# Graph attention and routed experts: a batch's moments placed ahead of the residual's, and the mask load issued inside the norms

## The chip, the cores and the metric

The kernel runs on one core of a Trainium2 chip. The metric is the time of one execution on the device in microseconds (us), as the median of several runs. The core has five instruction streams that this text names: TensorE (PE in the rows), VectorE (DVE), ScalarE (ACT), GpSimd (POOL) and SyncE (SP, which only issues transfers). They run beside one another and wait for one another through semaphores.

## The reference, cut to what matters

For each of 16 batches of 512 rows with 128 features:

```
xn   = layernorm(x)                          # first norm
Wh   = xn @ W.T;  si, sj = Wh @ a1, Wh @ a2
e    = leaky_relu(si[:, None] + sj[None, :], 0.2)
att  = softmax(where(adj > 0, e, -9e15))
x1   = x + elu(att @ Wh)                     # first residual
x2   = layernorm(x1)                         # second norm
rw   = softmax(mean over tokens of x2 @ Wr + br), rescaled, softmax again
out  = x1 + layernorm(x2 + sum over the top 2 experts of gate * (gelu(x2 @ W1 + b1) @ W2 + b2)) * gamma + beta
```

`adj` is an int32 matrix of 512 x 512 for every batch.

## The kernel before, in words

Partitions hold rows: a batch is four tiles of 128 rows. The program has two phases. Phase one runs the attention of the 16 batches and keeps x1 and the transposed x2 in SBUF. Then comes a short routing stage, and phase two runs the two chosen experts of each batch. The change touches phase one only.

Phase one is a software pipeline written out by hand, one list of calls per engine and step. `pipeline` writes some first steps out, puts steps 6 to 11 into a hardware loop (two steps to an iteration, with semaphore targets and addresses in registers) and writes the last ones out again. In step n each engine works on several batches at once:

- VectorE, step n: `masked_max` of batch n, tiles 2 and 3 (L690, mask plus the spread destination scores, with the row maximum); between them `residual_pos` of batch n-2 (L731); then `residual_neg` of batch n-2 (L739, writes x1), `stats2` of batch n-2 (L749, four BN_STATS that read x1), `stats1` of batch n+3 (L667, four BN_STATS on the coming rows), `make_mask` of batch n+1 (L676), `invert_sums` of batch n-1 (L711), `logits` tile 0 (L702), `normalize` of n-1 (L720), `logits` 1 and 2, `masked_max` of batch n+1 tiles 0 and 1, `logits` tile 3.
- GpSimd, step n: `norms(n + 2)`, `load_adj(n + 2)`, `row_shifts(n)`. `norms` turns the moments of two batches at once, the first norm of batch n+2 and the second norm of batch n-3, into reciprocal deviations (L457 to L485, the power at L485) and the bias nb (L491). It waits for both VectorE moments (semaphores bn1_stats and bn2_stats). `load_adj` (L436) waits until the mask of two batches back is made and issues the transfer of one batch's adj, cast from int32 to bf16 by the transfer. `row_shifts` (L503 to L514) waits for all four maxima of batch n, and works out z_max, shift_neg and shift_pos.
- ScalarE, step n: `copy_xnt` (L1130), `scale_x2` of batch n-3 (L1195, four instructions that need nb), `leaky_part` tiles 0 and 1 (L1154, need shift_neg), `copy_wh` (L1145, needs the first norm), leaky 2, `probs` (L1184, exponentials of the transposed logits), `copy_x2t` (L1202), leaky 3, probs 1 and 2, `exp_h` (L1162), probs 3.
- TensorE, step n: transposes of x2 (L1426) and of the logits (L1435), the spread of destination scores (L1412), transposes of x (L1389), `attend` (L1451), `project` (L1399).
- SyncE: loads of x and stores of x2 within SBUF.

`logits` of tile 0 waits for leaky of tile 0 and for shift_pos; `invert_sums` waits for the last `attend` of batch n-1. Ahead of the pipeline each engine has a head for batch 0: on GpSimd it ends with `load_adj(0, 2)`, `norms(0, 2)`, and the pipeline's first step then does `norms(0, 3)`, `load_adj(0, 3)`, `row_shifts(0, 1)`. The DMA queue of GpSimd carries nothing but adj in phase one.

A helper, `waits_met`, increments a semaphore of the engine's own behind the waits of a step.

Of the kernel before, what the change touches and what calls it, by code (L numbers as in the profile page):

```python
# [22 lines left out]
def batch_at(half, n):  # L23

    h = half + n // 2
    return 2 * h + n % 2, h, n % 2


def gat_moe_kernel(nc, x, adj, gnn_w, gnn_a, w_router, b_router, w1, b1, w2, b2, gamma, beta, out):
# [15 lines left out]
    with ExitStack() as ctx:  # L45
# [214 lines left out]
        def pipeline(engine, step, first, last, lead, lag):  # L260


            lo = first + lead + (first + lead) % 2
            hi = last - lag + 1
            hi -= hi % 2
            for i in range(first, lo):
                step(0, i)
            with engine.Fori(lo // 2, hi // 2) as half:
                step(half, 0)
                step(half, 1)  # L270
            for i in range(hi, last + 1):
                step(0, i)

        def in_range(half, n, last=B - 1):
            return not isinstance(half, int) or 0 <= 2 * half + n <= last
# [7 lines left out]
        FIRST, LAST = -4, 16  # L283
        LEAD, LAG = 10, 5
# [9 lines left out]
        def past(half, b, k):  # L294
            return not isinstance(half, int) or b >= k

        def waits_met(engine):


            engine.sem_inc(s_met[engine.engine], 1)  # L300
# [119 lines left out]
        def _(pool):  # L420
# [9 lines left out]
            def load_adj(half, n):  # L430

                b, h, par = batch_at(half, n)
                if past(half, b, 2):
                    pool.wait_ge(s_mask, b - 1)
                    waits_met(pool)
                nc.gpsimd.dma_start(adj_sb[par][:], adj_dram[b]).then_inc(s_adj[par], 16)  # L436

            def norms(half, n):
# [4 lines left out]
                first = in_range(half, n)  # L443
# [17 lines left out]
                if second:  # L461
                    nc.gpsimd.tensor_tensor(nm2[:], bn[:, 1, :, 1], bn[:, 1, :, 4], ALU.add).then_inc(s_n2, 1)
                pool.wait_ge(s_norm, base + 1)
                nc.gpsimd.tensor_tensor(sums[:, 3, kinds, :], sums[:, 1, kinds, :], sums[:, 1, kinds, :],
                                        ALU.mult).then_inc(s_norm, 1)
                pool.wait_ge(s_norm, base + 3)
                waits_met(pool)
                nc.gpsimd.tensor_scalar(sums[:, 2, kinds, :], sums[:, 2, kinds, :], 1.0 / D, LN_EPS, ALU.mult,
# [76 lines left out]
            def step(half, n):  # L545
                if in_range(half, n + 2, KEPT - 1 + NORM_LAG):
                    norms(half, n + 2)
                if in_range(half, n + 2) and past(half, n + 2, 2):
                    load_adj(half, n + 2)
                if in_range(half, n):  # L550
                    row_shifts(half, n)

# [7 lines left out]
            row_shifts(0, 0)  # L560
            load_adj(0, 2)
            norms(0, 2)
            pipeline(pool, step, 1, LAST, LEAD + FIRST - 1, LAG)
            pool.wait_ge(s_rw, 64)
            nc.gpsimd.tensor_scalar(br_sb[:], br_sb[:], float(N), 0.0, ALU.mult, ALU.add).then_inc(s_br, 1)
            norm2_third_last()
# [75 lines left out]
        def _(dve):  # L642
# [26 lines left out]
            def make_mask(half, n):  # L669

                b, h, par = batch_at(half, n)
                dve.wait_ge(s_adj[par], 16 * h + 16)
                if past(half, b, 1):
                    dve.wait_ge(s_md, T * b)
                waits_met(dve)
                nc.vector.tensor_scalar(mask[:], adj_sb[par][:], 0.0, -MASKED, ALU.is_le, ALU.mult).then_inc(s_mask, 1)  # L676
# [57 lines left out]
            def residual_neg(half, n):  # L734
                b, h, par = batch_at(half, n)
                dve.wait_ge(s_hexp, b + 1)
                dve.wait_ge(s_x1, 2 * b + 1)
                waits_met(dve)
                nc.vector.scalar_tensor_tensor(out=x1_all[:, b, :], in0=h_exp[:], scalar=1.0, in1=x1_part[:],  # L739
                                               op0=ALU.min, op1=ALU.add).then_inc(s_x1, 1)  # L740
# [36 lines left out]
            def step(half, n):  # L777
                if in_range(half, n):
                    masked_max(half, n, 2)
                if in_range(half, n - 2, B - 2):  # L780
                    residual_pos(half, n - 2)
                if in_range(half, n):
                    masked_max(half, n, 3)
                if in_range(half, n - 2, B - 2):
                    residual_neg(half, n - 2)
                if in_range(half, n - 2, END - 1):
                    stats2(half, n - 2)
                if in_range(half, n + 3):
                    stats1(half, n + 3)
                if in_range(half, n + 1):  # L790
                    make_mask(half, n + 1)
                if in_range(half, n - 1, B - 2):
                    invert_sums(half, n - 1)
                if in_range(half, n):
                    logits(half, n, 0)
                if in_range(half, n - 1, B - 2):
                    normalize(half, n - 1)
                if in_range(half, n):
                    logits(half, n, 1)
                if in_range(half, n):  # L800
                    logits(half, n, 2)
                if in_range(half, n + 1):
                    masked_max(half, n + 1, 0)
                if in_range(half, n + 1):
                    masked_max(half, n + 1, 1)
                if in_range(half, n):
                    logits(half, n, 3)
# [880 lines left out]
```

## Time and profile before

| what | value |
|---|---|
| median of 3 runs | 298.2 us (296.28 to 299.17) |
| the profiled execution, its own time | 298.8 us |
| its span, first to last instruction | 297.1 us |
| mean granted TensorE clock | 0.978 of full |
| PE busy | 260.7 us (88%) |
| DVE busy | 240.9 us (81%) |
| ACT busy | 229.7 us (77%) |
| POOL busy | 174.0 us (59%) |

The shares are means over two phases with different limits, so they do not say what bounds phase one. In the rows below, times count from the span's start. A row of the timeline gives the start, the length, the engine, the line, the operation with its tiles, how many instructions are merged into it, and in brackets how long the engine stood idle before it and which producer ended that.

### The profile page before, as it was taken

How to read it: one execution, taken by the hardware profiler on the slowest of the kernel's cores; microseconds unless marked ns; L12 is line 12 of the kernel's file. 1: busy time of each engine (PE TensorE's matmuls, PEld its weight loads, DVE VectorE, ACT ScalarE, POOL GpSimd, SP SyncE). 2: the span in 40 equal slices, each digit the busy share in tenths (PEclk: the TensorE clock that was granted, in tenths of full speed). 3: DMA queues.
4: the chain of work that ended last, by engine and by line, in shares of the span. 5: the costliest groups of instructions: out<-in, count | busy, mean ns of one | idle time of the engine just before them, and what ended most of it. 6: DMA issues, size and time to landing. Idle time of an engine off the chain costs nothing. (4 is left out here: it accounts for less than half of the span.)

```text
span 297.1 us, 7856 instructions
## 1 busy us (share of the span) xinstructions
PE 260.7 (88%) x1958; PEld 236.5 (80%) x1959; DVE 240.9 (81%) x689; ACT 229.7 (77%) x498; POOL 174.0 (59%) x392
## 2 busy tenths in 40 slices
PE   7585988998889888988898798999999999999990
PEld 5475978888879787978787685689999999999990
DVE  4595899999999999999889877466678787678766
ACT  2384678999988998899889775778779888788670
POOL 3688387787778777788845951123343244432375
PEclk9998699999999999999999899999999999999998
DMA  6998406337575577468500000465465555556313
GB/s 105 182 295 157 71 3 106 58 92 174 108 135 128 125 143 172 98 139 158 107 18 23 35 1 36 151 207 161 143 196 169 196 155 171 177 176 194 107 38 106
DMA packets 47069, 37.26 MB, mean 125 GB/s; under 512 B 2848, under 2 KB 41152, under 8 KB 47040
## 3 DMA queue, kind: packets, MB, share of 16 engines
q1 hardware_dynamic: 38176, 27.49, 29.1%
q0 software_dynamic: 8864, 9.45, 21.6%
q8 instruction: 11, 0.18, 0.2%
q14 instruction: 18, 0.15, 0.1%
HBM read 29.57 MB, written 4.20 MB: 114 GB/s over the span
## 5 line engine op out<-in xcount | busy, mean ns | idle before, releaser
L1451 PE MATMUL banks<-whx,prob_t 128*128 128x129 f32 x512 | 65.9, 278 | 0.0
L1451 PEld LDWEIGHTS banks<-whx,prob_t 128*128 128x128 f32 x512 | 62.1, 195 | 0.0
L1435 PE MATMUL banks<-ident,logit 128*128 128x128 f32 x256 | 40.7, 292 | 21.3 <-DVE logit L702 21.0
L1154 ACT ACTIVATE leaky<-masked_dst,shift_neg 128x512 f32<-128x512 f32 x64 | 44.7, 724 | 12.6 <-POOL shift_neg L513 12.6
L1435 PEld LDWEIGHTS banks<-ident,logit 128*128 128x128 f32 x256 | 29.5, 147 | 29.1 <-DVE logit L702 20.7
L702 DVE SCALAR_TENSOR_TENSOR logit<-masked_dst,shift_pos,leaky 128x512 f32<-128x512 f32 x64 | 46.9, 744 | 3.7 <-POOL shift_pos L514 2.1
L1184 ACT ACTIVATE prob_t<-banks 128x512 f32<-128x512 f32 x64 | 37.0, 609 | 11.0 <-PE banks L1435 10.9
L690 DVE CUSTOM_DVE_ANT_0 masked_dst<-mask,banks 128x512 f32<-128x512 bf16 x64 | 42.2, 682 | 2.1 <-PE banks L1412 1.0
L1320 ACT ACTIVATE logit<-logit,nb,rstd 128x128 f32<-128x128 f32 x60 | 24.8, 484 | 14.7 <-POOL nb L612 14.7
L607 POOL TENSOR_SCALAR veps<-mv 128x4 f32<-128x4 f32 x15 | 5.8, 387 | 48.4 <-DVE mv L1021 44.4
L1624 PEld LDWEIGHTS banks<-w2s,masked_dst 128*128 128x128 f32 x256 | 29.7, 192 | 1.2 <-issue 0.7
L1624 PE MATMUL banks<-w2s,masked_dst 128*128 128x128 f32 x256 | 30.0, 275 | 0.3 <-ACT w2s L1339 0.3
L1609 PE MATMUL banks<-x2t_hi,w_pair 128*128 128x512 f32 x64 | 26.8, 419 | 0.5 <-DMA w_pair<-w_parts 0.5
L1624 PEld LDWEIGHTS banks<-w2s,leaky 128*128 128x128 f32 x224 | 26.1, 192 | 0.6
L1624 PE MATMUL banks<-w2s,leaky 128*128 128x128 f32 x224 | 26.1, 275 | 0.0
L1003 DVE TENSOR_TENSOR logit<-banks,x_all 128x512 f32<-128x512 f32 x15 | 10.4, 691 | 19.2 <-ACT logit L1320 12.7
L485 POOL TENSOR_TENSOR rstd<-sums,minus_half 128x8 f32<-128x8 f32 (+1 forms) x17 | 24.6, 1449 | 1.4 <-ACT whx L1145 0.6
L1611 PE MATMUL banks<-x2t_hi,w_pair 128*128 128x512 f32 x64 | 25.3, 395 | 0.0
L1610 PE MATMUL banks<-x2t_lo,w_pair 128*128 128x512 f32 x64 | 24.9, 389 | 0.0
L1330 ACT ACTIVATE masked_dst<-banks,b_sel 128x512 f32<-128x512 f32 x32 | 19.7, 676 | 3.2 <-PE banks L1611 2.4
L1330 ACT ACTIVATE leaky<-banks,b_sel 128x512 f32<-128x512 f32 x32 | 19.8, 678 | 2.6 <-PE banks L1611 2.5
L1412 PE MATMUL banks<-ident,whx 128*128 128x128 f32 x128 | 19.3, 296 | 2.8 <-ACT whx L1145 2.5
(172 smaller groups left out, 580.4 us busy)
## 6 DMA issues: line engine op xcount, KB each, us to landing
adj_sb<-in_adj_dram POOLq DMA_DIRECT2D x16, 512.0 KB, 7.2
w_pair<-w_parts SPq DMA_DIRECT2D x31, 256.0 KB, 2.5
x_all<-in_x_dram SPq DMA_DIRECT2D x16, 256.0 KB, 4.6
w2r<-in_L_ffn_W_dram SPq DMA_DIRECT2D x32, 128.0 KB, 2.1
out_dram<-prob_t SPq DMA_DIRECT2D x15, 256.0 KB, 2.3
x_all<-x2s SPq DMA_DIRECT2D x13, 256.0 KB, 5.1
x_rows<-in_x_dram SPq DMA_DIRECT2D x8, 256.0 KB, 2.9
w_parts<-in_L_ffn_W_dram SPq DMA_DIRECT2D x1, 1024.0 KB, 8.8
```

What stands on the lines that cost most here:

```text
L690: nc.vector.tensor_tensor_reduce(out=masked_dst[:, t, :], in0=mask[:, t, :], in1=dst_ps, scale=1.0, scalar=-3e38, op0=ALU.add, op1=ALU.max ...
L702: nc.vector.scalar_tensor_tensor(out=logit[:, t, :], in0=masked_dst[:, t, :], scalar=shift_pos[:, t:t + 1], in1=leaky[:, t, :], op0=ALU.ad ...
L1154: nc.scalar.activation(leaky[:, t, :], masked_dst[:, t, :], ACT.Identity, bias=shift_neg[:, t:t + 1], scale=ALPHA).then_inc(s_leaky, 1)
L1184: nc.scalar.activation(prob_t[:, t, :], lt_ps[t % 2], ACT.Exp).then_inc(s_prob, 1)
L1320: nc.scalar.activation(zn[par][:, tile], zs[par][:, tile], ACT.Identity, bias=nb3[par][:, t:t + 1], scale=rstd3[par][:, t:t + 1]).then_inc ...
L1330: nc.scalar.activation(hidden[par][:, kc, :], hid_ps[kc], ACT.Gelu, bias=b1_sel[:, c, bass.ds(b * TOP_K + k, 1)]).then_inc(s_hid, 1)
L1435: last = nc.tensor.transpose(lt_ps[t % 2][:, c * P:(c + 1) * P], logit[:, t, c * P:(c + 1) * P], ident[:])
L1451: last = nc.tensor.matmul(into[:, 0:D + 1], prob_t[:, t, c * P:(c + 1) * P], whx[par][:, c, 2:WHX], start=(c == 0), stop=(c == T - 1))
L1609: nc.tensor.matmul(hid_ps[kc], lo, x2t_hi[par][:], start=True, stop=False)
L1610: nc.tensor.matmul(hid_ps[kc], hi, x2t_lo[par][:], start=False, stop=False)
L1611: nc.tensor.matmul(hid_ps[kc], hi, x2t_hi[par][:], start=False, stop=True).then_inc(s_hid_ps, 1)
L1624: last = nc.tensor.matmul(y_ps[par][:, t * D:(t + 1) * D], hidden[par][:, kc, t * P:(t + 1) * P], w2s[par][:, kc // FC, kc % FC, :], start ...
```

## The change

Three edits, two on GpSimd and one on VectorE. (1) From batch 4 on, `load_adj` of a batch is called inside `norms` of the same batch, behind the square (L464), and no longer between `norms` and `row_shifts`. (2) The first pipeline step of GpSimd is written out: `load_adj(0, 3)` stands behind `row_shifts(0, 1)`. (3) On VectorE `stats1` of batch n+3 is called ahead of `stats2` of batch n-2.

```diff
@@ norms
                 nc.gpsimd.tensor_tensor(sums[:, 3, kinds, :], sums[:, 1, kinds, :], sums[:, 1, kinds, :],
                                         ALU.mult).then_inc(s_norm, 1)
+                if first and past(half, n, 4):
+                    load_adj(half, n)
                 pool.wait_ge(s_norm, base + 3)
@@ step of GpSimd
                     norms(half, n + 2)
-                if in_range(half, n + 2) and past(half, n + 2, 2):
-                    load_adj(half, n + 2)
                 if in_range(half, n):
                     row_shifts(half, n)
@@ head of GpSimd
             norms(0, 2)
-            pipeline(pool, step, 1, LAST, LEAD + FIRST - 1, LAG)
+            norms(0, 3)
+            row_shifts(0, 1)
+            load_adj(0, 3)
+            pipeline(pool, step, 2, LAST, LEAD + FIRST - 2, LAG)
@@ step of VectorE
                     residual_neg(half, n - 2)
+                if in_range(half, n + 3):
+                    stats1(half, n + 3)
                 if in_range(half, n - 2, END - 1):
                     stats2(half, n - 2)
-                if in_range(half, n + 3):
-                    stats1(half, n + 3)
```

GpSimd, second batch: this is the end of `norms(0, 3)`, then what stands between it and `norms(0, 4)`. whx1 belongs to batch 1, adj_sb1 receives adj of batch 3. Before:

```order
L485 TENSOR_TENSOR rstd12_1<-sums12,minus_half 128x4
L436 DMA adj_sb1<-in_adj_dram 128x4x512
L503 TENSOR_SCALAR src_alpha<-whx1 128x4
L505 TENSOR_TENSOR z_max<-whx1,dst_max 128x4
L508 TENSOR_SCALAR z_alpha<-z_max 128x4
L509 TENSOR_SCALAR z_pos<-z_max 128x4
L511 TENSOR_TENSOR row_max<-z_pos,z_alpha 128x4
L513 TENSOR_TENSOR shift_neg<-src_alpha,row_max 128x4
L514 TENSOR_TENSOR shift_pos<-whx1,row_max 128x4
```

and with the change:

```order
L487 TENSOR_TENSOR rstd12_1<-sums12,minus_half 128x4
L505 TENSOR_SCALAR src_alpha<-whx1 128x4
L507 TENSOR_TENSOR z_max<-whx1,dst_max 128x4
L510 TENSOR_SCALAR z_alpha<-z_max 128x4
L511 TENSOR_SCALAR z_pos<-z_max 128x4
L513 TENSOR_TENSOR row_max<-z_pos,z_alpha 128x4
L515 TENSOR_TENSOR shift_neg<-src_alpha,row_max 128x4
L516 TENSOR_TENSOR shift_pos<-whx1,row_max 128x4
L436 DMA adj_sb1<-in_adj_dram 128x4x512
```

The issue has moved from ahead of the seven row-shift instructions to behind them.

GpSimd, a written-out step of the pipeline (the norms for batch 5): before, the issue stands between nb and src_alpha.

```order
L464 TENSOR_TENSOR sums12<-sums12 128x8
L468 TENSOR_SCALAR sums12<-sums12 128x8
L470 TENSOR_SCALAR sums12<-sums12 128x8
L473 TENSOR_TENSOR sums12<-sums12 128x8
L478 TENSOR_SCALAR nm2<-nm2 128x4
L485 TENSOR_TENSOR rstd12_1<-sums12,minus_half 128x8
L491 TENSOR_TENSOR nb2_1<-nm2,rstd12_1 128x4
L436 DMA adj_sb1<-in_adj_dram 128x4x512
L503 TENSOR_SCALAR src_alpha<-whx1 128x4
```

With the change it stands behind the square:

```order
L464 TENSOR_TENSOR sums12<-sums12 128x8
L436 DMA adj_sb1<-in_adj_dram 128x4x512
L470 TENSOR_SCALAR sums12<-sums12 128x8
L472 TENSOR_SCALAR sums12<-sums12 128x8
L475 TENSOR_TENSOR sums12<-sums12 128x8
L480 TENSOR_SCALAR nm2<-nm2 128x4
L487 TENSOR_TENSOR rstd12_1<-sums12,minus_half 128x8
L493 TENSOR_TENSOR nb2_1<-nm2,rstd12_1 128x4
L505 TENSOR_SCALAR src_alpha<-whx1 128x4
```

The issue went ahead of six instructions of `norms`, nb and the power among them; src_alpha now follows nb directly.

VectorE, step 2 (x_all under L739 and L749 is x1 of batch 0, under L667 the rows of batch 5). Before:

```order
L739 SCALAR_TENSOR_TENSOR x_all<-h_exp,x_part 128x512
L749 BN_STATS bn_1<-x_all 128x6 x4
L667 BN_STATS bn_1<-x_all 128x6 x4
L676 TENSOR_SCALAR mask<-adj_sb 128x2048
L711 RECIPROCAL inv_sum<-banks 128x4
```

and with the change:

```order
L742 SCALAR_TENSOR_TENSOR x_all<-h_exp,x_part 128x512
L670 BN_STATS bn_1<-x_all 128x6 x4
L752 BN_STATS bn_1<-x_all 128x6 x4
L679 TENSOR_SCALAR mask<-adj_sb 128x2048
L714 RECIPROCAL inv_sum<-banks 128x4
```

The two groups of four have changed places; nothing is added or taken away.

## Rows read from the trace of the kernel before

**Rows 1.** Busy time by stretch: the hardware loop of phase one.

```profile
69.00:127.00 58.00, 51.42 (x432) 48.01 (x432) 55.98 (x151) 52.47 (x121) 45.47 (x109) 1.00 0.63 134
```

**Rows 2.** Waits of VectorE, 30 to 185 us: total, times, longest.

```profile
DVE bn L749 <- DVE x_all L739: 2.3, 11, 0.2
...
DVE masked_dst L690 <- PE banks L1412: 1.0, 1, 1.0
```

**Rows 3.** Timeline of VectorE, a written-out step (step 3).

```profile
46.60 0.69 DVE L739 SCALAR_TENSOR_TENSOR x_all<-h_exp,x_part 128x512 f32<-128x512 f32 x1
47.43 0.87 DVE L749 BATCH_NORM_STATS2 bn<-x_all 128x6 f32<-128x128 f32 x4
...
48.99 0.68 DVE L676 TENSOR_SCALAR mask<-adj_sb 128x2048 bf16<-128x2048 bf16 x1
49.59 0.17 DVE L711 RECIPROCAL inv_sum<-banks 128x4 f32<-128x4 f32 x1
49.68 0.72 DVE L702 SCALAR_TENSOR_TENSOR logit<-masked_dst,shift_pos,leaky 128x512 f32<-128x512 f32 x1
...
50.92 1.40 DVE L702 SCALAR_TENSOR_TENSOR logit<-masked_dst,shift_pos,leaky 128x512 f32<-128x512 f32 x2
```

**Rows 4.** Timeline of VectorE in the hardware loop (step 11).

```profile
123.48 0.69 DVE L739 SCALAR_TENSOR_TENSOR x_all<-h_exp,x_part 128x512 f32 x1
124.40 0.87 DVE L749 BATCH_NORM_STATS2 bn<-x_all 128x6 f32 x4 [0.24 <-DVE x_all L739]
```

**Rows 5.** Timeline of TensorE: the last attend of step 3 and of step 13.

```profile
48.09 1.06 PE L1451 MATMUL banks<-whx,prob_t 128*128 128x129 f32 x8
...
144.26 1.06 PE L1451 MATMUL banks<-whx,prob_t 128*128 128x129 f32 x8
```

**Rows 6.** Timeline of VectorE, step 13, where it waits for TensorE and ScalarE.

```profile
145.43 0.18 DVE L711 RECIPROCAL inv_sum<-banks 128x4 f32<-128x4 f32 x1 [0.34 <-PE banks L1451]
146.00 0.75 DVE L702 SCALAR_TENSOR_TENSOR logit<-masked_dst,shift_pos,leaky 128x512 f32<-128x512 f32 x1 [0.39 <-ACT leaky L1154]
```

**Rows 7.** Timeline of ScalarE: scale_x2 and leaky of step 3, leaky of step 13.

```profile
46.57 1.65 ACT L1195 ACTIVATE x2s<-x_all,nb,rstd 128x128 f32<-128x128 f32 x4
48.52 1.33 ACT L1154 ACTIVATE leaky<-masked_dst,shift_neg 128x512 f32<-128x512 f32 x2 [0.30 <-POOL shift_neg L513]
...
145.18 1.33 ACT L1154 ACTIVATE leaky<-masked_dst,shift_neg 128x512 f32<-128x512 f32 x2 [0.79 <-POOL shift_neg L513]
```

**Rows 8.** Timeline of GpSimd: around the issue of step 3, and a z_max of the loop.

```profile
45.06 0.20 POOL L491 TENSOR_TENSOR nb<-nm,rstd 128x4 f32<-128x4 f32 x1
45.57 0.84 POOL L436 DMA_DIRECT2D adj_sb<-in_adj_dram  x1 [0.31 <-issue]
...
46.76 0.58 POOL L505 TENSOR_TENSOR z_max<-whx,dst_max 128x4 f32<-128x4 f32 x1
...
50.58 0.20 POOL L464 TENSOR_TENSOR sums<-sums 128x8 f32<-128x8 f32 x1
...
124.20 0.19 POOL L505 TENSOR_TENSOR z_max<-whx,dst_max 128x4 f32<-128x4 f32 x1
```

**Rows 9.** Timeline of GpSimd at the start of the pipeline (step 1).

```profile
24.70 0.84 POOL L436 DMA_DIRECT2D adj_sb<-in_adj_dram  x1
25.57 0.60 POOL L503 TENSOR_SCALAR src_alpha<-whx 128x4 f32<-128x4 f32 x1
```

**Rows 10.** The same stretch on VectorE.

```profile
28.33 0.75 DVE L702 SCALAR_TENSOR_TENSOR logit<-masked_dst,shift_pos,leaky 128x512 f32<-128x512 f32 x1 [2.12 <-POOL shift_pos L514]
```

**Rows 11.** One-us stretch: busy PE, PEld, DVE, ACT, POOL; granted clock; DMA share.

```profile
28.00:29.00 1.00, 0.00 (x0) 0.00 (x0) 0.67 (x1) 1.00 (x3) 0.73 (x3) 0.57 1.21 199
```

**Rows 12.** The line of the adj issue: length min/median/max in ns; its landing.

```profile
L436 POOL DMA_DIRECT2D adj_sb<-in_adj_dram x16: 798/852/969, 2.1 to 141.8; - x16
...
DMA to landing us min/median/max: 5.4/7.2/10.0
```

**Rows 13.** Timeline of GpSimd, the head: its most stretched small instruction.

```profile
21.38 1.18 POOL L459 TENSOR_TENSOR sums<-bn 128x4 f32<-128x4 f32 x1
```

## The prediction

> **What bounds the kernel now.** I read the busy time by stretch first, then the waits of VectorE, then the timelines of the four engines over one step, each against VectorE's. In the hardware loop VectorE is busy 55.98 of 58 us, ahead of ScalarE (52.47), TensorE (51.42) and GpSimd (45.47) [rows 1]. So phase one costs what VectorE's list of instructions costs, plus the few places where it stands still. The largest sum of those is a wait for itself: stats2 (L749) reads what residual_neg (L739) has just written, 2.3 us in 11 places [rows 2]. What the reader is to see in the timeline is the distance between starts, because an instruction that waits for nothing starts before the one ahead has fully ended: the mask of 0.68 us starts at 48.99 and the reciprocal at 49.59, 0.60 later. From L739 to L749 it is 46.60 to 47.43, 0.83, in a written-out step [rows 3], and 123.48 to 124.40, 0.92, in the loop [rows 4]. The second place is at the start: tile 0 of the logits of batch 1 waits 2.12 us for GpSimd's row shifts [rows 10], and ahead of those shifts stands an adj issue of 0.84 us [rows 9]. Phase two is not touched and keeps its length.
>
> **Edit 3, stats1 ahead of stats2.** Same instructions, other order. stats1 reads rows loaded long before, so it can start 0.60 behind L739; by the time its four instructions are through, L739 has long been written, and stats2 waits for nothing. Gain in a written-out step: 0.83 - 0.60 = 0.23; in the loop 0.92 - 0.60 = 0.32. Steps 2 to 12 have both groups: five written out (2 to 5 and 12) and six in the loop. Steps 13 and 14 have no coming rows and keep the wait. What is late next? Four neighbours, in the written-out step with L739 as zero:
> - Reciprocal (now at 2.99) needs the last attend. That ends at 48.09 + 1.06 = 49.15, which is 2.55. In step 13, where VectorE does wait for it, the attend ends at 145.32 [rows 5] and the reciprocal starts at 145.43 [rows 6], 0.11 later. So the reciprocal may start at 2.66; the new order brings it to 2.76. Margin 0.10.
> - Logits tile 0 (now 3.08) needs leaky tile 0. In step 13 leaky starts at 145.18 [rows 7] and the waiting logits at 146.00 [rows 6], 0.82 later. Here leaky starts at 48.52, 1.92, so logits may start at 2.74; the new order wants 2.85. Margin 0.11.
> - In the loop z_max starts 0.72 behind L739 (123.48 and 124.20 [rows 4, 8]), not 0.16 as at 46.76, and ends at 0.91 instead of 0.74 (46.76 + 0.58). Its start is late because the adj issue stands ahead of src_alpha. Left so, leaky and with it the logits would be late by up to 0.17, which is more than the margin; edit 1 takes the issue away from there.
> - GpSimd's norms start when both groups are through, which is now earlier by the same 0.23 to 0.32.
>
> So the gain fits under its neighbours, with a tenth of a microsecond to spare. Sum: 5 x 0.23 + 6 x 0.32 = 3.1 us. For the loop I take 0.30 instead of 0.32, since there both margins are used up almost wholly: 3.0 us. Bounds: 0 (every step finds another wait at once) and 3.1.
>
> **Edit 1, the issue inside the norms.** It adds nothing; it moves 0.84 us, and the 0.31 us ahead of it [rows 8], past the power and nb. In the new place the square ends 1.10 us behind the start of logits tile 0 (50.58 + 0.20 against 49.68 [rows 3, 8]), the issue starts at 1.41 and ends at 2.26. The two instructions that come next, L468 and L470, ran until now beside logits 1 and 2, which are busy until 52.32, that is 2.64 [rows 3]. Small GpSimd instructions are stretched there: z_max takes 0.58 us beside L739 and 0.19 us clear of it [rows 8]. The issue itself never took over 0.97 us in 16, wherever VectorE was [rows 12]. So it mostly fills time in which L468 and L470 were held, and these run short behind it. They start at 2.30 instead of 1.29 and are free from 2.64 on. I put nb about 0.3 us later than now against the logits. ScalarE wants nb for scale_x2 at 46.57, and nb ends at 45.26: 1.31 us of cover [rows 7, 8], 1.0 left. Behind nb, src_alpha starts about 0.9 us earlier (0.31 + 0.84 gone, 0.3 given back), so z_max has only its maxima to wait for. Its own worth is nothing where the issue was covered (written-out steps) and the 0.17 us of the loop's z_max otherwise, which is already in the term above. Nobody waits for the landing: it takes 10.0 us at most [rows 12], and the issue moves earlier against the mask that needs it. Bounds of this edit by itself: nothing, as long as the cover holds; what it costs if not is rival 4.
>
> **Edit 2, the second batch.** Batch 1's row shifts lose the issue ahead of them: they start at 24.75 instead of 25.57. src_alpha took 0.60 us there against 0.20 of its kind, with a mask of VectorE beside it; started earlier it may be clear of that, but a later one of the chain can meet the mask instead. VectorE and ScalarE both stand idle for that chain, so it counts in full: at least 0.82, at most 0.82 + 0.40 = 1.22; I take 1.0. Batch 3's adj is issued some 2 to 3 us later than at 24.70, by 27.7, and is needed by the mask of step 2, one step before the one at 48.99; even a landing of 10.0 us [rows 12] makes that. norms(0, 4) stands behind it, and GpSimd then waits for logits of batch 1 in any case.
>
> **Sum.** 3.0 + 1.0 = 4.0 us. Against the profiled execution 298.8 - 4.0 = 294.8. Its own time lies 0.6 us over the median, so against the median: 298.2 - 4.0 = 294.2 us, -1.3%. About 1% is what a measurement of this kernel can tell from no change (its three runs are 2.9 us apart), so this is a gain just past what shows.
>
> **Rivals.**
> 1. *Another wait takes the place of the one removed, in the loop.* The margins of 0.10 and 0.11 were read in a written-out step. In the loop the targets are computed in registers, and every wait costs a little more (0.92 against 0.83 between L739 and L749 is a sign of it). If the reciprocal or the logits there wait for TensorE or ScalarE, or VectorE's own issuing sets the pace, the six loop steps give nothing: 4.0 - 6 x 0.30 = 2.2, 296.0 us. For it: margins of a tenth. Against: VectorE shows 96% busy there, so it is its instructions that count.
> 2. *Only the start is gained.* The steps are held by a ring through another engine, and VectorE's wait merely sits inside it: 298.2 - 1.0 = 297.2. Against it: in the middle steps no wait but L749's own recurs in VectorE's list.
> 3. *The clock goes better.* In the stretch 28 to 29 us, with nothing for TensorE to do in it, its granted clock is 0.57 [rows 11], that is mostly the lower of its two levels (2.4 and 1.2 GHz), and VectorE then waits 1.0 us for the spread scores, the only such wait [rows 2]. With the row shifts earlier, that idle time is shorter by 1.0; if the clock stays up, that wait goes too: 294.2 - 1.0 = 293.2.
> 4. *Slower: the issue is held by VectorE.* Its new place is beside two instructions with two SBUF operands. The same kind of company has stretched a small GpSimd instruction from 0.20 to 1.18 us [rows 13], 5.9 times. If the issue stretched so, it would take 5.0 us. An issue of up to 1.25 us ends before logits 2 does and delays nothing more; 1.0 us of cover follows. So past 2.3 us each of the 12 steps that hold an issue inside norms pays one for one, and from 2.3 + 4.0 / 12, some 2.6 us, the change loses. At 5.0 us that is 12 x 2.7 = 32 us, 326 us; half way between the least and this, at 3.2 us, it is 12 x 0.9 = 10.8, 305.0 us, at which I price it. Against it: all 16 issues lie between 0.80 and 0.97 [rows 12] though they too stood where VectorE was never idle.
>
> The Trainium skill speaks for rival 4: "SBUF — State Buffer", section "SBUF: two separate sides", warns that a transfer issued from GpSimd has its descriptors written by that engine, and that VectorE instructions which take the shared port pair lock it out; its example goes from about 620 to about 3100 ns. By that factor of five the issue here would take some 4.2 us, an estimate from that page, and the change would lose. The rows disagree so far: a maximum of 0.97 us in 16.
>
> **How the numbers follow.** The forecast has 0.55, rival 1 has 0.2, rival 2 0.1, rival 3 0.1, rival 4 0.05. Faster by over 1% (under 295.2) are the forecast, less a fifth of it for the scatter, and rival 3, with a little of rival 1: 0.57. Within 1%: the rest of the forecast, rivals 1 and 2: 0.37. Slower: rival 4 and a remainder: 0.06. The range goes from 292.8 (rival 3, with the upper end of edit 2 and 0.2 of scatter) to 297.4 (rival 2).
>
> **What would show it.** In the trace of the changed kernel: L749's wait for L739 gone from VectorE's waits except in steps 13 and 14; L739 to mask 2.16 us in all steps from 2 to 12; the period of a loop step down by 0.3; the first logits of batch 1 at about 27.3 instead of 28.33; the issue still at 0.85 us, and L468 and L470 behind it no longer stretched (near 0.2 us). New rows among VectorE's waits, for TensorE at the reciprocal or for leaky at the logits, of over 0.1 us a step, would mean rival 1. An issue of over 2.6 us would mean rival 4. I would be wrong altogether if the stretch from L739 to the logits did not shrink.

## The result, and the profile after

| | before | after |
|---|---|---|
| median of 6 runs | 297.76 us (296.28 to 299.17) | 301.82 us (299.55 to 302.47) |
| the profiled execution, its own time | 298.8 us | 301.32 us |
| its span | 297.1 us | 299.5 us |
| mean granted TensorE clock | 0.978 | 0.978 |

The ratio after to before is 1.013, with a 95% interval of 1.0099 to 1.0162. The change makes the kernel slower by 1.3%; 294.2 us had been predicted, with a range that ended at 297.4. The two profiled executions lie 2.5 us apart and the medians 4.1, so the rows tell where the time goes, not quite how much.

All lines of the changed kernel stand 2 or 3 further down: L742 is `residual_neg` (L739 before), L752 `stats2` (L749), L670 `stats1` (L667), L693 `masked_max`, L705 `logits`, L714 the reciprocal, L1157 leaky, L1148 `copy_wh`, L1415 the spread, L1454 `attend`.

The busy time of the loop's stretch, which answers to [rows 1] (the same columns):

```profile
69.00:127.00 58.00, 50.09 (x416) 47.46 (x415) 51.76 (x139) 50.02 (x113) 41.89 (x102) 0.97 0.62 126
```

VectorE has gone from 55.98 us of work in this stretch to 51.76, so it now stands still for 6.2 of 58 us. Its waits, which answer to [rows 2]:

```profile
DVE bn L670 <- DMA x_rows<-in_x_dram: 5.0, 6, 1.8
DVE logit L705 <- POOL shift_pos L516: 1.4, 1, 1.4
...
DVE masked_dst L693 <- issue: 1.2, 1, 1.2
```

The wait of `stats2` for `residual_neg` has gone, as predicted: 0.3 us in two places is left. In its place stands a wait that the trace of before did not have at all: `stats1` waits six times, 5.0 us in all, for a DMA, the load of the coming rows. The line for `shift_pos` is the wait at the start, 2.1 us before.

VectorE in the steps of the loop, which answers to [rows 4]:

```profile
82.95 0.69 DVE L742 SCALAR_TENSOR_TENSOR x_all<-h_exp,x_part 128x512 f32 x1
84.33 0.88 DVE L670 BATCH_NORM_STATS2 bn<-x_rows 128x6 f32<-128x128 f32 x4 [0.69 <-DMA x_rows<-in_x_dram]
...
93.11 0.69 DVE L742 SCALAR_TENSOR_TENSOR x_all<-h_exp,x_part 128x512 f32 x1
95.61 0.87 DVE L670 BATCH_NORM_STATS2 bn<-x_rows 128x6 f32<-128x128 f32 x4 [1.82 <-DMA x_rows<-in_x_dram]
...
101.72 0.69 DVE L693 CUSTOM_DVE_ANT_0 masked_dst<-mask,banks 128x512 f32<-128x512 bf16 x1 [1.22 <-issue]
...
105.42 0.69 DVE L742 SCALAR_TENSOR_TENSOR x_all<-h_exp,x_part 128x512 f32 x1
106.50 0.88 DVE L670 BATCH_NORM_STATS2 bn<-x_rows 128x6 f32<-128x128 f32 x4 [0.39 <-DMA x_rows<-in_x_dram]
```

Read the tile's name: in the loop `stats1` reads `x_rows`, a pair of buffers that is filled on the way, while in steps 2 to 4 it reads `x_all`, filled long before. From 93.11 to 105.42 a step takes 12.31 us. The second wait in it, put down to "issue", is one for TensorE, as its timeline shows together with GpSimd's and SyncE's:

```profile
87.62 0.86 POOL L436 DMA_DIRECT2D adj_sb<-in_adj_dram  x1
...
90.76 0.37 SPq L317 DMA_DIRECT2D x_rows<-in_x_dram  x1
...
98.71 1.11 PE L1438 MATMUL banks<-ident,logit 128*128 128x128 f32 x4 [2.61 <-DVE logit L705]
...
99.62 1.92 PE L1415 MATMUL banks<-ident,whx 128*128 128x128 f32 x8
```

TensorE stood idle for 2.61 us behind the late rows. Then the eight spread matmuls took 1.92 us, against 1.16 in step 3, and the masked maximum had to wait for them. The granted clock (last column but two) says why, and the stretch at the row load what was going on there:

```profile
92.00:94.00 2.00, 2.00 (x20) 2.00 (x20) 1.80 (x4) 1.87 (x5) 1.37 (x3) 1.00 1.16 293
...
98.00:100.00 2.00, 1.29 (x6) 1.29 (x7) 2.00 (x4) 0.24 (x2) 1.92 (x5) 0.63 0.00 0
100.00:102.00 2.00, 2.00 (x12) 2.00 (x11) 0.78 (x2) 1.65 (x4) 1.82 (x5) 0.51 0.70 64
```

At 92 to 94 us the DMA engines move 293 GB/s, while the rows are on their way. At 100 to 102 us the clock is at 0.51, the lower of its two levels.

The same step before, by contrast (VectorE needs the rows at 96.14, 4.13 us behind the issue of their load):

```profile
92.01 0.37 SPq L317 DMA_DIRECT2D x_rows<-in_x_dram  x1
...
94.42 0.69 DVE L739 SCALAR_TENSOR_TENSOR x_all<-h_exp,x_part 128x512 f32 x1
95.35 0.87 DVE L749 BATCH_NORM_STATS2 bn<-x_all 128x6 f32 x4 [0.24 <-DVE x_all L739]
96.14 0.86 DVE L667 BATCH_NORM_STATS2 bn<-x_rows 128x6 f32<-128x128 f32 x4
```

The line of the row load, from issue to landing, before and after:

```profile
DMA to landing us min/median/max: 2.7/2.9/5.7
```

```profile
DMA to landing us min/median/max: 2.8/3.3/4.6
```

The largest value of before, 5.7 us, belongs to a load at 58.38 us that nothing waits for. Of the six loads for steps 7 to 12, the ones that matter, the landing takes 2.7 to 2.9 us before and 2.8 to 4.6 after, 3.4 at the median. Every waiting `stats1` starts 0.16 to 0.24 us behind the landing of its rows.

The account on VectorE, read from its timelines and waits: from `residual_neg` of step 2 to that of step 13 it is 105.64 us before (37.12 to 142.76) and 109.73 after (35.57 to 145.30), 4.09 more. The rows cost 5.0 and the spread 1.2; 2.0 of the waits for `residual_neg` are gone. That makes 4.2. Ahead of step 2 the new kernel had won 1.55 us. The four steps from 2 to 6 wait for no rows; they take 9.47 to 9.49 us each, and 9.47 to 9.48 before: there the exchange on VectorE has brought nothing.

### The profile page after: what moved, and what is told of

It is laid out like the page before. It is cut to its first block and busy times, and to the rows that moved or that the text cites. A ratio compares the mean times of both kernels' runs of the same rounds, so it can differ in the third digit from the quotient of the medians.

```text
span 299.5 us, 7860 instructions
## 1 busy us (share of the span) xinstructions
PE 262.0 (87%) x1959; PEld 237.5 (79%) x1959; DVE 240.8 (80%) x689; ACT 230.5 (77%) x498; POOL 171.1 (57%) x392
## 3 DMA queue, kind: packets, MB, share of 16 engines
q0 software_dynamic: 8864, 9.45, 21.4%
## 5 line engine op out<-in xcount | busy, mean ns | idle before, releaser
L1454 PE MATMUL banks<-whx,prob_t 128*128 128x129 f32 x512 | 66.0, 278 | 0.0
L1454 PEld LDWEIGHTS banks<-whx,prob_t 128*128 128x128 f32 x512 | 62.2, 195 | 0.0
L1157 ACT ACTIVATE leaky<-masked_dst,shift_neg 128x512 f32<-128x512 f32 x64 | 44.6, 723 | 10.8 <-POOL shift_neg L515 10.8
L705 DVE SCALAR_TENSOR_TENSOR logit<-masked_dst,shift_pos,leaky 128x512 f32<-128x512 f32 x64 | 47.1, 747 | 3.3 <-POOL shift_pos L516 1.4
L693 DVE CUSTOM_DVE_ANT_0 masked_dst<-mask,banks 128x512 f32<-128x512 bf16 x64 | 42.2, 682 | 2.4 <-issue 1.2
L1198 ACT ACTIVATE x2s<-x_all,nb,rstd 128x128 f32<-128x128 f32 (+1 forms) x52 | 21.4, 489 | 0.0
```

Of the source, the lines that this page charges most:

```text
L693: nc.vector.tensor_tensor_reduce(out=masked_dst[:, t, :], in0=mask[:, t, :], in1=dst_ps, scale=1.0, scalar=-3e38, op0=ALU.add, op1=ALU.max ...
L705: nc.vector.scalar_tensor_tensor(out=logit[:, t, :], in0=masked_dst[:, t, :], scalar=shift_pos[:, t:t + 1], in1=leaky[:, t, :], op0=ALU.ad ...
L1157: nc.scalar.activation(leaky[:, t, :], masked_dst[:, t, :], ACT.Identity, bias=shift_neg[:, t:t + 1], scale=ALPHA).then_inc(s_leaky, 1)
L1454: last = nc.tensor.matmul(into[:, 0:D + 1], prob_t[:, t, c * P:(c + 1) * P], whx[par][:, c, 2:WHX], start=(c == 0), stop=(c == T - 1))
```

## The experiments

Every kernel below was timed in three rounds beside the kernel before on the same chip; the ratio is to that. None of them leaves anything out. Edits 1, 2 and 3 are the three of the change.

**Which edit does it?** The possible causes were these: the exchange wants the rows sooner than they can be there; the moved adj transfer crowds their load; the moved issue delays something on GpSimd; and, for the gain that did not come, a ring through the other engines. The theories in the expectations, each under a letter, are variants of these, each with the time that it foresaw. Where a theory puts the whole loss on edit 1, edit 3 alone must bring the predicted 3 us.

Edit 3 alone:

```diff
                     residual_neg(half, n - 2)
+                if in_range(half, n + 3):
+                    stats1(half, n + 3)
                 if in_range(half, n - 2, END - 1):
                     stats2(half, n - 2)
-                if in_range(half, n + 3):
-                    stats1(half, n + 3)
```

> Edit 3 alone. Theory R (ring and late rows): in the written-out steps the period stays 9.47 us, because a ring over the row shifts, leaky, copy_wh and the spread scores has the same length as VectorE's list; in the loop stats1 comes 0.9 us sooner to rows whose load was issued only some 2.8 us ahead of it and takes 2.8 to 3.0 us, so it waits 0.2 to 0.5 us in 7 steps, most of it inside the slack of 0.2 to 0.3: no change to +0.8 us, 297.8 to 298.8. Theory C (crowding: the loss comes from the moved adj transfer, which slows the load of the rows): no wait for the rows of over 0.1 us here, 3 us faster than before. Theory N (my first sum): 3 us faster.

Measured: 296.99 us against 297.35, ratio 0.998 (0.9947 to 1.0013). The 3 us are not there, so neither the first sum nor the theory that lays everything on edit 1 holds. The same step as above:

```profile
92.89 0.69 DVE L739 SCALAR_TENSOR_TENSOR x_all<-h_exp,x_part 128x512 f32 x1
93.78 0.87 DVE L667 BATCH_NORM_STATS2 bn<-x_rows 128x6 f32<-128x128 f32 x4 [0.20 <-DMA x_rows<-in_x_dram]
```

With the issue in its old place `stats1` waits 0.2 to 0.3 us for the rows, 1.2 us in five steps, not up to 1.8. The loop steps take 9.5 to 9.8 us, hardly less than before. Here the load is issued at 90.55 and adj only behind it, at 92.19; in the changed kernel adj went out 3.1 us ahead of the load.

Edit 1 alone:

```diff
@@ norms, behind the square
+                if first and past(half, n, 4):
+                    load_adj(half, n)
@@ step of GpSimd
-                if in_range(half, n + 2) and past(half, n + 2, 2):
+                if isinstance(half, int) and n + 2 == 3:
                     load_adj(half, n + 2)
```

> Edit 1 alone (the third issue stays ahead of the row shifts). Theory R: the rows land in 3.3 to 4.6 us instead of 2.9, but stats1, in its old place, has 3.9 to 4.1 us: nearly no wait, no change within 0.5 us, or up to 1 us faster in the loop since z_max no longer starts 0.72 behind the residual. Theory G (the issue itself holds up GpSimd's norms): 2 to 4 us slower.

Measured: 297.67, ratio 1.0011 (0.9984 to 1.0038). The landing of the rows shows the other half of the cause:

```profile
DMA to landing us min/median/max: 2.9/3.4/4.9
```

They take 3.4 us now at the median, but with `stats1` in its old place only one step waits, for 1.0 us. That step, number 8, is long all the same: 11.78 us against 9.63 before, with the wait for the spread behind it as in the changed kernel (1.1 us, the clock at 0.50 from 100 to 102 us). Other loop steps are shorter than before, two of them 9.48 us, as the expectation had allowed for. Each edit spends a part of the same slack, and neither overdraws it often. Together they do, in every step from 7 to 12.

Edit 2 alone:

```diff
             norms(0, 2)
-            pipeline(pool, step, 1, LAST, LEAD + FIRST - 1, LAG)
+            norms(0, 3)
+            row_shifts(0, 1)
+            load_adj(0, 3)
+            pipeline(pool, step, 2, LAST, LEAD + FIRST - 2, LAG)
```

> Edit 2 alone. The first logits of batch 1 start 0.7 us earlier; if TensorE's clock then stays at its upper level for the spread scores, 1.5 us in all: 296.3 to 297.1. All theories agree here; it gives the size of this term.

Measured: 296.48, ratio 0.9973 (0.9937 to 1.001): 0.8 us less, with zero not excluded. In its profile the clock falls at 28 to 32 us and once more at 41 to 46, and a step of 10.42 us stands there; part of what the start gains is given back so.

Edits 1 and 2, the change without its exchange:

```diff
@@ the changed kernel, step of VectorE
-                if in_range(half, n + 3):
-                    stats1(half, n + 3)
                 if in_range(half, n - 2, END - 1):
                     stats2(half, n - 2)
+                if in_range(half, n + 3):
+                    stats1(half, n + 3)
```

> Edits 1 and 2 without edit 3. Theory R: the whole loss is stats1 in its new place meeting rows that land late, so without it the sum of the two other runs remains: 1 to 2 us faster than before, 295.8 to 296.8. Theory G: still slower than before.

Measured: 297.24, ratio 0.9988 (0.9958 to 1.0018), and 295.8 to 296.8 had been expected: the gain of 1 to 2 us did not come. But the loss is gone with the exchange, though the transfers still crowd (landing 3.1/3.5/4.6 us). It takes both.

Edits 1 and 2, with the exchange only where the rows come from `x_all`:

```diff
+                early_rows = isinstance(half, int) and n + 3 < DIRECT
+                if early_rows:
+                    stats1(half, n + 3)
                 if in_range(half, n - 2, END - 1):
                     stats2(half, n - 2)
-                if in_range(half, n + 3):
+                if in_range(half, n + 3) and not early_rows:
                     stats1(half, n + 3)
```

> The changed kernel with stats1 ahead of stats2 only in the steps whose rows lie in x_all from early on (batches under 8); in the loop and behind it the old order. Theory L: no long wait for rows is left, the time is that of edits 1 and 2, 297.2, about 4 us faster than the changed kernel, and the ring makes the swap itself worth nothing.

Measured: 296.14 against 297.5, ratio 0.996 (0.9926 to 0.9995), 1.1 us under the 297.2 expected, with one wait for rows of 0.6 us. The exchange does no harm where the rows are there.

Edits 2 and 3, the issue in its old place:

```diff
@@ the changed kernel, norms
-                if first and past(half, n, 4):
-                    load_adj(half, n)
@@ step of GpSimd
+                if in_range(half, n + 2) and past(half, n + 2, 2):
+                    load_adj(half, n + 2)
```

> Edits 2 and 3, the issue left where it was. Theory L: waits for the rows of about 1.2 us in all, as in the run of edit 3 alone, within the slack of the steps; time as with edit 2 alone, 296 to 297. If any early stats1 is costly whatever the issue does: over 299.

Measured: 296.6 against 297.8, ratio 0.9983 (0.9952 to 1.0015), two waits for rows of 0.5 us in all and two of 0.4 us in all put down to "issue", in which `stats1` starts just as far behind the landing.

With this the cause can be read from four kernels that all have edit 2 and differ only in edits 1 and 3. In step 8 the load of the rows takes 4.5 to 4.9 us in each of the four kernels with edit 1 timed here, and 2.8 to 3.0 in before and in the ones with edits 2 or 3 alone or together. Why it is this step that is lengthened most was not tried.

**Take the late rows away.** The rows of all 16 batches are loaded straight into `x_all`, ahead of time; `x_rows` and the hardware loop of phase one are not used. Once with the order of before and once with all three edits:

```diff
-        s_xd = [sem(f"x_loaded_direct{i}") for i in range(8)]
+        s_xd = [sem(f"x_loaded_direct{i}") for i in range(16)]
-        DIRECT = 8
+        DIRECT = 16
@@ pipeline
+            if lead + lag > 8 or first + lead > 5:
+                for i in range(first, last + 1):
+                    step(0, i)
+                return
```

> The kernel before with all 16 batches of rows loaded straight into their own place well ahead (no x_rows buffers) and phase one written out in full, which the static addresses need. Its steps should all take the 9.47 us of the written-out ones instead of 9.6 to 9.8 in the loop: 1 to 1.5 us faster, 296. If fetching the longer program costs, slower.

> The changed kernel in the same form: all three edits, but rows that are never late. Theory L (the loss is stats1 waiting for late rows, which needs edits 1 and 3 together): no wait for x, and the time is that of rows_before less what edit 2 gives, 0 to 1.5 us faster than rows_before. Theory G (the order on the engines costs by itself): 3 to 4 us slower than rows_before. Ring: the period stays 9.47 though stats2 no longer waits.

Measured: 298.4 and 296.53 against 297.8; ratios 1.0031 (0.9993 to 1.0069) and 0.9962 (0.9928 to 0.9996). With all three edits and no late rows the kernel is no slower than before, and 1.9 us faster than the same form in the old order (0 to 1.5 had been expected): that settles the loss. In the second none of VectorE's waits in phase one is for rows. From 30 to 165 us the largest, and what is left for `residual_neg`, are:

```profile
DVE inv_sum L718 <- PE banks L1458: 1.8, 3, 1.2
...
DVE bn L756 <- DVE x_all L746: 0.3, 2, 0.2
```

The steps take 9.47 to 9.49 us in either order (one of 10.48 at a fall of the clock). So even with the rows there, and without the wait of `stats2`, the exchange does not shorten a step.

The first of the two kernels missed its expectation: 1 to 1.5 us less were expected, and 0.6 more came. Its phase one is indeed shorter: steps 6 to 11 take 56.88 us instead of 58.27, and `residual_neg` of step 11 starts at 121.61, 1.87 ahead of before (0.83 of it won ahead of step 2). In its profiled execution, which took 300.08 us and so 1.7 more than the median, the loss lies behind that, where phase two starts. VectorE in the kernel before, then in this one:

```profile
194.69 1.29 DVE L986 TENSOR_TENSOR x_all<-x_all,b_mix 128x512 f32<-128x512 f32 x2 [3.76 <-DMA b_mix<-b_spread]
...
203.08 0.69 DVE L1003 TENSOR_TENSOR logit<-banks,x_all 128x512 f32<-128x512 f32 x1 [3.58 <-PE banks L1624]
```

```profile
192.00 1.29 DVE L990 TENSOR_TENSOR x_all<-x_all,b_mix 128x512 f32<-128x512 f32 x2 [3.21 <-DMA b_mix<-b_spread]
...
204.43 0.69 DVE L1007 TENSOR_TENSOR logit<-banks,x_all 128x512 f32<-128x512 f32 x1 [6.57 <-PE banks L1628]
```

From 2.69 us ahead it falls to 1.35 behind. TensorE and the clock in that stretch:

```profile
196.06 0.50 PE L1613 MATMUL banks<-x2t_hi,w_pair 128*128 128x512 f32 x1 [1.90 <-DMA w_pair<-w_parts]
...
198.10 0.63 PE L1613 MATMUL banks<-x2t_hi,w_pair 128*128 128x512 f32 x1
...
198.00:202.00 4.00, 4.00 (x21) 3.37 (x21) 0.00 (x0) 2.66 (x5) 2.04 (x4) 0.71 0.48 151
```

TensorE waits 1.90 us for the second pair of expert weights, 0.51 before; then the clock falls, and matmuls that take 0.39 us before take 0.63. The kernel with all three edits in this form waits 1.12 us there and keeps its clock. So in this execution the form pays for its better loop at the start of phase two. Why the weights come later was not tried, and whether they do in every execution isn't shown.

**What holds a step, if not VectorE's wait?** Step 3 of the changed kernel, VectorE, ScalarE and TensorE:

```profile
45.05 0.69 DVE L742 SCALAR_TENSOR_TENSOR x_all<-h_exp,x_part 128x512 f32<-128x512 f32 x1
...
47.90 0.72 DVE L705 SCALAR_TENSOR_TENSOR logit<-masked_dst,shift_pos,leaky 128x512 f32<-128x512 f32 x1
...
49.13 1.60 DVE L705 SCALAR_TENSOR_TENSOR logit<-masked_dst,shift_pos,leaky 128x512 f32<-128x512 f32 x2
...
50.82 0.69 DVE L693 CUSTOM_DVE_ANT_0 masked_dst<-mask,banks 128x512 f32<-128x512 bf16 x1
...
46.98 1.33 ACT L1157 ACTIVATE leaky<-masked_dst,shift_neg 128x512 f32<-128x512 f32 x2 [0.29 <-POOL shift_neg L515]
48.22 1.13 ACT L1148 ACTIVATE whx<-banks,rstd 128x130 f32<-128x130 f32 x4
...
49.39 1.16 PE L1415 MATMUL banks<-ident,whx 128*128 128x128 f32 x8
```

From the start of `residual_neg` the first logits have come 0.23 us nearer (3.08 before [rows 3], now 2.85), just as predicted. But logits 1 and 2 now take 1.60 us, not 1.40, because the second of them needs leaky of tile 2, which has not moved (4.17 behind `residual_neg`, 4.16 before). Nothing that follows has moved either: leaky starts at 1.93 (1.92 before [rows 7]), `copy_wh` at 3.17 (before 49.76 - 46.60 = 3.16), the spread at 4.34 (4.35), the next batch's first masked maximum at 5.77 (5.76). This looks like a ring, a chain of waits through several engines that comes back to where it began, one batch on: the last masked maximum of a batch, GpSimd's row shifts, leaky, `copy_wh`, the spread on TensorE, the first masked maximum of the next batch, and from it through VectorE's list to the last. Its wait is on ScalarE: 0.29 us for shift_neg. Test: shorten the row shifts, by the same maximum in another form, which takes one instruction less and lets shift_neg follow z_pos directly (the edit in short; each line is one GpSimd instruction).

```diff
-  src_alpha = ALPHA * src
+  src_alpha = (1 - ALPHA) * src
   z_max = src + dst_max
-  z_alpha = ALPHA * z_max
+  z_alpha = -ALPHA * dst_max
   z_pos = (1 - ALPHA) * max(z_max, 0)
-  row_max = z_pos + z_alpha
-  shift_neg = src_alpha - row_max
-  shift_pos = src - row_max
+  shift_neg = z_alpha - z_pos
+  shift_pos = src_alpha + shift_neg
```

First in the kernel before, with VectorE's wait left in:

> The kernel before with a shorter row-shift chain on GpSimd: shift_neg = -0.2 dst_max - 0.8 max(z, 0), shift_pos = 0.8 src + shift_neg, the same values by six instructions, shift_neg about 0.4 us sooner. Ring theory: in the kernel before, two things are equally long, the ring and VectorE's own list, so shortening the ring alone leaves the written-out period at 9.47: no change within 0.5 us. If the ring alone bound the step, the period would fall by 0.2 to 0.4 and the time by 3 us.

Measured: 294.19 against 297.8, ratio 0.9918 (0.9868 to 0.9968): the expectation missed, it allowed 0.5 us. Written-out steps with both groups take 9.38 to 9.45 us instead of 9.47: the ring was a little longer than VectorE's list with its wait in it, so it was the ring that set the pace. But by the profiles steps 2 to 12 give only 1.0 us. Steps 13 and 14, at which the expectation had not looked, give 1.6: they take 9.18 and 9.39 us instead of 9.98 and 10.22, for it was there that the logits waited for leaky and leaky 0.79 us for shift_neg [rows 6, 7]. A further 1.7 us lies behind step 15, where the profile of before has one more fall of the clock (0.52 at 168 to 170 us) that this one has not.

Then with the rows loaded straight and all three edits:

```diff
@@ the kernel with direct rows and all three edits, row_shifts
+  the shorter form above
```

> All three edits, rows never late, and the shorter row-shift chain. Ring theory: now neither the ring nor VectorE's list holds the step at 9.47 us; the period should fall to between 9.2 (VectorE's list without the wait) and 9.3 in steps 2 to 12, 2 to 3 us faster than rows_after, 293.5 to 294.5. If another wait is equally long, the period stays at 9.4.

Measured: 291.66 against 297.5, ratio 0.9793 (0.9734 to 0.9851), less than the 293.5 expected at least: steps 13 and 14 gain here too (9.14 and 9.37 us). Its steps 6 and 7, from one `residual_neg` to the next:

```profile
71.35 0.69 DVE L745 SCALAR_TENSOR_TENSOR x_all<-h_exp,x_part 128x512 f32<-128x512 f32 x1
...
80.59 0.68 DVE L745 SCALAR_TENSOR_TENSOR x_all<-h_exp,x_part 128x512 f32<-128x512 f32 x1
...
89.72 0.69 DVE L745 SCALAR_TENSOR_TENSOR x_all<-h_exp,x_part 128x512 f32<-128x512 f32 x1
```

9.24 and 9.13 us, where it was 9.47 to 9.49 without the shorter row shifts and 9.38 to 9.45 with them but without the exchange. Now the exchange pays. That is what shows the ring: each of the two alone gains little or nothing in a step, and together they gain 0.2 to 0.3 us.

The same without edit 1:

```diff
@@ norms
-                if first and past(half, n, 4):
-                    load_adj(half, n)
@@ step of GpSimd
+                if in_range(half, n + 2) and past(half, n + 2, 2):
+                    load_adj(half, n + 2)
```

> The same with the adj issue in its old place, between nb and the row shifts. Tells what edit 1 is worth once nothing waits for rows. In written-out steps src_alpha follows the issue in time for z_max, so the same time as rows_after_short within 0.5 us; if the shortened step makes GpSimd's own list late, up to 2 us slower.

Measured: 290.11 against 297.5, ratio 0.9745 (0.9692 to 0.9798), with steps 4 to 11 of 9.16 to 9.19 us (9.72 and 9.91 in steps 2 and 3, 9.54 in step 12). The median is 1.55 us lower than with edit 1, not within 0.5 as expected, but the executions, four of each kernel, overlap (290.74 to 293.09 and 289.59 to 291.17). Edit 1 brings nothing here either; whether it costs something is open.

Last, the simplest version, with the loop and `x_rows` as before: edits 2 and 3 and the shorter row shifts.

```diff
@@ the kernel with edits 2 and 3, row_shifts
+  the shorter form above
```

> Edits 2 and 3 and the shorter chain with the loop and the x_rows buffers as before. Theory L: the shorter step brings stats1 still closer to the landing of its rows, so the loop gains little: written-out steps 9.2 to 9.3, loop steps 9.5; 293 to 294.5.

Measured: 290.63 against 297.5, ratio 0.9764 (0.9707 to 0.982), again under the 293 to 294.5 expected. Written-out steps take 9.15 to 9.21 us, loop steps 9.27 to 9.57, steps 13 and 14 9.15 and 9.38.

```profile
186.26 1.29 DVE L988 TENSOR_TENSOR x_all<-x_all,b_mix 128x512 f32<-128x512 f32 x2 [3.80 <-DMA b_mix<-b_spread]
...
194.56 0.69 DVE L1005 TENSOR_TENSOR logit<-banks,x_all 128x512 f32<-128x512 f32 x1 [3.33 <-PE banks L1626]
```

Here phase two starts as in the kernel before, 8.3 us from the first line to the second, 8.4 there and about 10 in the version of 290.11. Hence a slower loop ends at the same time. Both beat the kernel before by some 7 us; between them the measurement does not decide.

The two pairs of edits side by side (ratios to before). All four kernels of the first table have edit 2:

| | issue between norms and row shifts | issue inside norms |
|---|---|---|
| `stats2` first | 0.9973 | 0.9988 |
| `stats1` first | 0.9983 | 1.013 |

| | row shifts of before | shorter row shifts |
|---|---|---|
| `stats2` first | 1 | 0.9918 |
| `stats1` first, edit 2 | 0.9983 | 0.9764 |

## Why the prediction was wrong, point by point

The step that failed is the term of edit 3, 3.0 of the 4.0 us forecast: it rests on rows "loaded long before", which they are not in the loop, and on four neighbours after which nothing else would hold the step. The first error turns the gain into a loss, with edit 1's transfer beside it; the second would have left no gain even without the loss.

- **Edit 3, "stats1 reads rows loaded long before, so it can start 0.60 behind L739".** True in steps 2 to 6, where it starts 0.60 behind: 45.05 and 45.66. False in steps 7 to 12. From step 5 on the rows come from `x_rows`, and that load can only go out when TensorE's transpose has freed the buffer: in step 8 at 92.01, 2.41 us ahead of L739. There its landing takes 2.8 us, and `stats1` starts 0.24 behind a landing; it had 4.13 us for the two and with the exchange has 2.41 + 0.60 = 3.0, so nothing was to spare. The name of the tile in VectorE's rows and the line of the row load would have told this; neither was read. This is the step from which the sign of the result comes: in place of 2.0 us of waits for `residual_neg` between steps 2 and 13 the kernel has 5.0 us of waits for rows, and 1.2 us more at the spread behind the longest of them.
- **Edit 3, the gain of 0.23 a step.** The wait went, but the time did not. Of the four neighbours checked the last on VectorE is logits 0, and they held: the reciprocal and logits 0 came at 2.75 and 2.85, as worked out. A fifth neighbour, the next batch's first masked maximum, was not checked, and it hangs on the spread, `copy_wh`, leaky and shift_neg, none of which starts from VectorE's moments. The 0.30 us that ScalarE waits for shift_neg stand in [rows 7]. Rival 2, "the steps are held by a ring through another engine", was right on this for the written-out steps, at a chance of 0.1. The argument against it, that no other wait recurs on VectorE, is not enough: where the ring is as long as the engine's list with its own wait in it, the engine shows only its own wait.
- **Edit 1, "nobody waits for the landing".** Nobody waits for the landing of adj. But its transfer, issued some 3 us ahead of the row load and no longer behind it, now overlaps the row load, and in steps 7 to 12 the landing of that load goes from 2.7 to 2.9 us up to 2.8 to 4.6. What the prediction left out was not a wait for the moved transfer but its company. Priced at nothing by itself, edit 1 does cost nothing measurable by itself (1.0011), one long step aside. Its working on GpSimd held: nb ends 0.2 us later against the logits (5.26 us behind their start in step 3 instead of 5.05), where about 0.3 had been estimated.
- **Edit 2, 1.0 us.** VectorE's wait fell from 2.12 to 1.42 us, and the logits start at 27.66 instead of 28.33: 0.67. src_alpha ran in 0.19 us, but z_pos then took 0.70 beside the mask, the possibility that the text named and the lower bound of 0.82 left out. In this profile the wait for the spread scores at the start is gone, too, as rival 3 had it (1.55 us ahead at step 2), and the clock falls some 2 us later. Neither is shown to be the edit's doing: the kernel with edit 2 alone has this wait (1.0 us, 0.66 ahead at step 2), and the one with edit 3 alone, whose start is that of before, has neither the wait nor the fall (1.29 ahead). Alone the edit measures 0.8 us with zero in its interval; its exact size stays open.
- **Rival 4, an issue held by VectorE.** It does not happen: the 16 issues last 0.78 to 0.97 us after, 0.80 to 0.97 before. The Trainium skill's "SBUF — State Buffer", section "SBUF: two separate sides", says that GpSimd cannot write the descriptors of its transfers while VectorE runs an operation in a two-port mode; of operations with two SBUF inputs it says that they lock out a GpSimd operation only if that one reads SBUF. The prediction had stretched the first rule to the second kind. For the second kind, the logits beside the new place, the trace shows no lengthening; it does not test the first. (The price of 305.0 us was taken at an issue of 3.2 us and called half way; half way between 2.3 and 5.0 would be 3.65. Nothing hangs on it.)

The line of the issue after, beside [rows 12]:

```profile
L436 POOL DMA_DIRECT2D adj_sb<-in_adj_dram x16: 782/865/969, 2.1 to 140.0; - x16
```

- **The slower side** had 0.06, all of it on rival 4 and a remainder. The loss came from a mechanism that was not among the rivals: a consumer moved forward, and a transfer moved onto the load that it reads.

## What to carry to other kernels

When a consumer (an instruction that reads a loaded buffer) moves forward, look up in the trace for each step which buffer it reads, when that buffer's load is issued and what frees it; written-out steps and loop steps can differ. When a DMA issue moves, look not only at who waits for it but at which other load is then in flight. And a wait on the busiest engine is worth what it shows only if the ring through the other engines is shorter: follow the chain on to the same instruction of the next batch, past the first neighbours that hold.

## What was not expected of the hardware

- The adj transfer (int32 in, bf16 out) issued some 3 us ahead of the row load lengthens it: the median landing of the row load is 2.9 us with the issue in its old place and 3.3 to 3.5 with edit 1. A third transfer, the load of x for the residual, follows the row load by 0.7 to 0.9 us in every one of these kernels, so it does not make the difference. In step 8 `stats1` could start 3.23 us behind the issue of the load (90.55 to 93.78) with edit 3 alone and 4.85 us (90.76 to 95.61) with all three.
- A short idle time of TensorE can cost a second time: behind 2.61 us of idleness the clock was at 0.51 and the spread matmuls took 1.92 instead of 1.16 us. Such falls, of about 1 us each, stand at different places in the profiles of kernels whose order is the same there (28, 30, 41, 168, 196 us); the one at 98 us stands only in the two kernels whose step 8 is longest. The time of an execution goes with the clock: of the kernel before beside the experiments, 15 executions with a mean granted clock of 0.978 took 297.48 to 299.26 us, and 14 with 0.989 or 0.990 took 296.0 to 297.43. So a reading from one profile can be off by a fall or two. What sets off a fall in one execution and not in the next isn't shown.
- A step of the hardware loop took 9.6 to 9.8 us before, the same work written out 9.47.
